# The second batch's queries loaded between the context pieces of the first batch, in a three-part transformer kernel on one core

## The chip, the cores and the metric

The kernel runs on one core of a Trainium2 chip. The metric is the device time of one execution in microseconds, the median of several executions. Times inside the kernel come from one profiled execution, counted from the start of its span.

## The reference

The program computes three sublayers in float32 on `x`, 8 batches of 64 rows of 2048. What matters here is the first of them:

```python
def _L0_xattn_ref(query, key):
    a = jnp.einsum('bqd,bkd->bqk', query, key)
    e = jax.nn.softmax(a, axis=-1)
    c = jnp.einsum('bqk,bkd->bqd', e, key)
    return c

x = x + _L0_xattn_ref(_layernorm(x, axis=-1), ctx_4096)
x = x + _L0_attn_ref(_layernorm(x, axis=-1), w_q, w_k, w_v, w_o)
x = x + _L0_ffn_ref(_layernorm(x, axis=-1), A_w, B_w, Wq_w, keys)
```

The context `ctx_4096` has 8 batches of 1601 rows of 2048; it serves as keys and as values. The second sublayer is a causal self-attention with 32 query and 8 key heads, the third a gated low-rank feed-forward; the change touches neither.

## The kernel before, in words

**Cross attention.** A batch's 1601 context rows are split into two halves of 833 and 768 rows (`TILES`), and a half is a stage, so there are 16 stages. The 2048 columns are split into four pieces of 512. Piece (x, c) is half x, columns c; it is one buffer `raw[x][:, c]` in SBUF with a semaphore of its own, `raw_in[x][c]`. A stage takes eight steps (`PER`), two per piece. At step t TensorE transposes two 128-column chunks of the half (`transpose_step`, line 637), one for ScalarE and one for VectorE to copy out of PSUM into `ct` (lines 445 and 587), and then multiplies the queries with the chunks that step t-1 transposed (`scores`, lines 673 and 676). Before the transposes of step t TensorE waits until both copies of step t-1 are done (lines 716 and 717). From the second stage on the steps also carry the products of the probabilities with the stage before's context (line 703). Steps 0 to 7 work on half 0 of batch 0, steps 8 to 15 on half 1.

**Queries.** `xq` holds a batch's 64 rows of `x`. For batch 0 VectorE normalizes them at once; TensorE transposes them behind the transposes of step 0 (`first_queries`, line 658, which adds one to `first_q_done`), and ScalarE copies them out (line 422). After that `xq` is free for batch 1. VectorE takes up a next batch's queries inside its loop over the steps of the batch before: after the copies of steps 3 and 4 the row statistics (`STATS_AT`, line 489, half of the columns in each), at steps 5 and 6 the chain for the inverse root, at steps 7 and 8 the normalization (line 499). At step 3 it first waits for the load:

```python
                    if at == STATS_AT[0]:
                        dve.wait_ge(xq_in, 16 * (b + 2))
```

The statistics of step 3 stand in VectorE's program behind the copy of step 3 and ahead of the copy of step 4. TensorE transposes the new queries at steps 13 and 14 (`Q_AT`, line 646).

**Loads.** All loads are issued by SyncE in program order (`cross_sync`, lines 363 to 418), on one queue. It issues the queries of batch 0, then the eight pieces of batch 0 in the order (0,0) to (0,3), (1,0) to (1,3), each from the third on after the piece two before it has landed, then the residual rows `xr` (the same rows of `x`, added to the output of the attention), and then it goes through the steps. At step 1 it waits for `first_q_done` and issues the queries of batch 1. A piece of half 0 takes three DMAs (128 partitions, 64 partitions and one row), a piece of half 1 one, `load_rows` one. Pieces of batch 1 are issued as the products of batch 0 release the buffers.

**The rest.** The decoder (self-attention and feed-forward, from line 800 on) follows on each engine behind the cross attention. Its first weight loads are issued at steps 100 and 106.

Of the kernel before, what the change touches and what calls it, by code (L numbers as in the profile page):

```python
# [16 lines left out]
NCOL = D // 512  # L17
# [82 lines left out]
def groups_before(t, ago):  # L100

    return GROUPS_AT.get(t - ago, [])
# [26 lines left out]
def evacuations(t):  # L129

    return min(t, STEPS) + 1
# [93 lines left out]
def cross_attention(nc, stack, x_rows, ctx, x1, x1_norm, ps, ident, ident_ready, x1_tiles, x1_ahead, row_bn,  # L225
# [5 lines left out]
    def keys_of(b, x, c, k0, k1, p0, p):  # L231
        lo = KEY0[x] + k0 * P + p0
        return ctx[b, lo:lo + (k1 - k0) * p, c * 512:(c + 1) * 512].rearrange("(k p) n -> p k n", p=p)
# [3 lines left out]
    def sb(name, shape, dt=F32):  # L237
        size = 4
        for n in shape[1:]:
            size *= n  # L240
        t = nc.alloc_sbuf_tensor_at(name, shape, dt, offset=here[0])
        here[0] += (size + 31) // 32 * 32
        return t

    def sem(name):
        return stack.enter_context(nc.semaphore(name))
# [3 lines left out]
    xq = sb("xa_xq", [P, D])[0:LQ, :]  # L250
# [36 lines left out]
    xq_in = sem("xa_xq_in")  # L287
# [5 lines left out]
    first_q_done = sem("xa_first_q_done")  # L293
# [24 lines left out]
    def column(c):  # L318
        return slice(c * 512, (c + 1) * 512)
# [8 lines left out]
    def both(eng, sems, n):  # L328

        for s in sems:  # L330
            eng.wait_ge(s, n)

    def group_over(h, c):
        return uses_before(h) + GROUP_END[h % HALVES][c] + 1
# [28 lines left out]
    def cross_sync(sp, aside):  # L363
        def load_piece(b, x, c):
            for k0, k1, p0, p in loads[x]:
                sp.dma_start(raw[x][p0:p0 + p, c, k0:k1, :], keys_of(b, x, c, k0, k1, p0, p)).then_inc(raw_in[x][c], 16)

        def load_rows(b, dst, s):
            sp.dma_start(dst[:], x_rows[b * LQ:(b + 1) * LQ, :]).then_inc(s, 16)

        load_rows(0, xq, xq_in)
        order = [(x, c) for x in range(HALVES) for c in range(NCOL)]
        for n, (x, c) in enumerate(order):
            if n >= 2:
                px, pc = order[n - 2]
                sp.wait_ge(raw_in[px][pc], 16 * len(loads[px]))
            load_piece(0, x, c)
        load_rows(0, xr, xr_in)
        for t in range(ALL_STEPS):
            if t == 1:  # L380
                sp.wait_ge(first_q_done, 1)
                load_rows(1, xq, xq_in)
            if t % (HALVES * PER) == Q_AT[1] + 1:
                b = t // (HALVES * PER) + 1
                if b + 1 < B:
                    both(sp, t_done, evacuations(t - 1))
                    load_rows(b + 1, xq, xq_in)
            for h, c in groups_before(t, 1):
                b, x = divmod(h, HALVES)
                both(sp, pv_done, group_over(h, c))  # L390
                if b + 1 < B:
                    load_piece(b + 1, x, c)
                elif x == 0 and c == 0:
                    for i in range(NCOL):
                        sp.wait_ge(stored[i], 16 * (B - 1))
                    sp.dma_start(x1_tiles[RT - 1][0:LQ, :], x1[(B - 2) * LQ:(B - 1) * LQ, :]).then_inc(sixth_in, 16)
                elif x == 0 and c == 1:
                    sp.wait_ge(norm_stored, 16 * (B - 2))
                    for r in range(RT - 1):
                        sp.dma_start(x1_ahead[r][:], x1_norm[r * P:(r + 1) * P, :]).then_inc(ahead_in[r], 16)  # L400
            for h, c in groups_before(t, 2):
                b, x = divmod(h, HALVES)
                if x == 1 and b + 1 < B:
                    sp.wait_ge(finished, NCOL * b + c + 1)
                    sp.dma_start(x1[b * LQ:(b + 1) * LQ, column(c)], xr[:, column(c)]).then_inc(stored[c], 16)
            if t in STORE_AT:
                b = STORE_AT[t]
                sp.wait_ge(out_norm, 2 * (b + 1))
                sp.dma_start(x1_norm[b * LQ:(b + 1) * LQ, :], xr[:]).then_inc(norm_stored, 16)
            if t in NEXT_AT:  # L410
                b = NEXT_AT[t]
                if b < B - 2:
                    sp.wait_ge(norm_stored, 16 * (b + 1))
                for c in range(NCOL):
                    sp.wait_ge(stored[c], 16 * (b + 1))
                load_rows(b + 1, xr, xr_in)
            if t in WEIGHT_LOAD_AT:
                aside(sp, WEIGHT_LOAD_AT.index(t))
# [313 lines left out]

    over = Over(pv_done, uses_before(STAGES), finished, ahead_in, stored)
    return over, (cross_sync, cross_scalar, cross_vector, cross_tensor)


# [1013 lines left out]
```

## Time and profile before

| | before |
|---|---|
| median of 3 executions | 1733.93 us (1732.92 to 1733.97) |
| profiled execution: device time | 1732.88 us |
| profiled execution: span | 1731.1 us |
| TensorE (PE) matmul busy | 1670.8 us |
| VectorE (DVE) busy | 560.9 us |
| ScalarE (ACT) busy | 455.4 us |
| GpSimd (POOL) busy | 372.5 us |
| mean granted clock of TensorE | 0.992 |

The span runs from the first to the last recorded instruction; the device time has a little more around it. PE are matmuls and transposes (a transpose is a matmul against the identity), SPq is SyncE's queue of DMA issues. In a timeline a row is a run of like instructions: start, duration, engine, line, operation, tiles, count, and in brackets the idle time before it with what ended it. A granted clock of 1.00 is 2.4 GHz, 0.50 is 1.2 GHz.

### The profile page before, as it was taken

How to read it: one execution, taken by the hardware profiler on the slowest of the kernel's cores; microseconds unless marked ns; L12 is line 12 of the kernel's file. 1: busy time of each engine (PE TensorE's matmuls, PEld its weight loads, DVE VectorE, ACT ScalarE, POOL GpSimd, SP SyncE). 2: the span in 40 equal slices, each digit the busy share in tenths (PEclk: the TensorE clock that was granted, in tenths of full speed). 3: DMA queues.
4: the chain of work that ended last, by engine and by line, in shares of the span. 5: the costliest groups of instructions: out<-in, count | busy, mean ns of one | idle time of the engine just before them, and what ended most of it. 6: DMA issues, size and time to landing. Idle time of an engine off the chain costs nothing.

```text
span 1731.1 us, 21539 instructions
## 1 busy us (share of the span) xinstructions
PE 1670.8 (97%) x9037; PEld 1224.9 (71%) x9037; DVE 560.9 (32%) x1018; ACT 455.4 (26%) x630; POOL 372.5 (22%) x95
## 2 busy tenths in 40 slices
PE   4899999999999979999999999999999999999999
PEld 3555555555555538888888878888888788887877
DVE  2445546365463451101202202103012022138423
ACT  1223332333333323231121221222212212232221
POOL 0000000000001002434434344343443443350010
PEclk9899999999999999999999999999999999999999
DMA  9166665757677543323233223223223342220023
GB/s 335 46 198 193 209 209 187 225 171 232 194 225 244 173 136 122 98 73 97 75 95 97 76 94 97 77 93 96 90 88 88 97 145 74 98 98 25 25 73 122
DMA packets 178882, 224.51 MB, mean 130 GB/s; under 512 B 4240, under 2 KB 102544, under 8 KB 176048
## 3 DMA queue, kind: packets, MB, share of 16 engines
q1 hardware_dynamic: 178816, 223.56, 40.9%
q8 instruction: 50, 0.82, 0.2%
q14 instruction: 16, 0.13, 0.0%
HBM read 212.54 MB, written 11.01 MB: 129 GB/s over the span
## 4 chain that ended last, share of the span: by engine, by line
PE 93%; DMA 2%; DVE 2%; ACT 1%; issue 1%; SPq 0%; DVEq 0%; ACTq 0%
PE ps L763 19%; PE ps L765 18%; PE ps L764 18%; PE ps L637 11%; PE ps L673 10%; PE ps L703 10%; PE ps L1487 2%; PE ps L1601 1%; DMA xa_raw_a<-in_ctx 1%; PE ps L1508 1%; DMA xa_xq<-in_x 1%; PE ps L646 1%; PE ps L1456 0%; DMA xa_raw_b<-in_ctx 0%; PE ps L1494 0%
## 5 line engine op out<-in xcount | busy, mean ns | idle before, releaser
L1071 POOL TENSOR_TENSOR w_lo<-raw,w_hi 128x2048 fp32r<-128x2048 f32 x75 | 345.1, 4602 | 647.8 <-ACT w_hi L1123 647.8
L763 PE MATMUL ps<-h_hi,w_hi 128*128 128x512 f32 x800 | 316.8, 396 | 0.0
L765 PE MATMUL ps<-h_hi,w_lo 128*128 128x512 f32 x800 | 312.1, 390 | 0.0
L764 PE MATMUL ps<-h_lo,w_hi 128*128 128x512 f32 x800 | 312.0, 390 | 0.0
L1307 DVE TENSOR_TENSOR rows<-rows,ps 128x512 f32<-128x512 f32 x128 | 87.9, 687 | 427.5 <-PE ps L765 427.5
L763 PE MATMUL ps<-w_hi,o_hi 128*128 128x512 f32 x528 | 208.1, 394 | 6.1 <-ACT sa_q_t L1158 4.1
L587 DVE COPY xa_ct<-ps 128x768 f32<-128x768 f32 (+1 forms) x128 | 126.8, 990 | 258.0 <-PE ps L637 174.1
L1123 ACT ACTIVATE w_hi<-raw 128x2048 fp32r<-128x2048 f32 x75 | 143.5, 1914 | 240.4 <-PE ps L765 240.4
L765 PE MATMUL ps<-w_hi,o_lo 128*128 128x512 f32 x528 | 205.8, 390 | 0.0
L764 PE MATMUL ps<-w_lo,o_hi 128*128 128x512 f32 x528 | 205.7, 390 | 0.0
L673 PE MATMUL ps<-xa_ct,xa_q_t 128*64 128x384 f32 x1024 | 203.3, 508 | 0.0
L445 ACT ACTIVATE xa_ct<-ps 128x768 f32<-128x768 f32 (+1 forms) x128 | 107.3, 838 | 331.0 <-PE ps L637 228.6
L763 PEld LDWEIGHTS ps<-h_hi,w_hi 128*128 128x128 f32 x800 | 150.6, 188 | 34.5 <-ACT sa_v_t L1158 2.0
L765 PEld LDWEIGHTS ps<-h_hi,w_lo 128*128 128x128 f32 x800 | 150.4, 188 | 31.8
L764 PEld LDWEIGHTS ps<-h_lo,w_hi 128*128 128x128 f32 x800 | 150.7, 188 | 29.8
L637 PEld LDWEIGHTS ps<-ident,xa_raw_a 128*128 128x128 f32 (+1 forms) x896 | 98.9, 145 | 74.8 <-issue 72.3
L637 PE MATMUL ps<-ident,xa_raw_a 128*128 128x128 f32 (+1 forms) x896 | 111.6, 276 | 28.7 <-DVE xa_ct L587 15.2
L637 PEld LDWEIGHTS ps<-ident,xa_raw_b 128*128 128x128 f32 x768 | 82.8, 140 | 59.3 <-issue 54.8
L1076 POOL TENSOR_TENSOR w_lo<-raw,w_hi 128x2048 fp32r<-128x2048 f32 x2 | 9.4, 4698 | 535.2 <-ACT w_hi L986 535.2
L763 PEld LDWEIGHTS ps<-w_hi,o_hi 128*128 128x128 f32 x528 | 99.2, 188 | 29.4 <-ACT sa_q_t L1158 6.7
L765 PEld LDWEIGHTS ps<-w_hi,o_lo 128*128 128x128 f32 x528 | 99.2, 188 | 20.8
L764 PEld LDWEIGHTS ps<-w_lo,o_hi 128*128 128x128 f32 x528 | 99.3, 188 | 19.7
(205 smaller groups left out, 1530.4 us busy)
## 6 DMA issues: line engine op xcount, KB each, us to landing
xa_raw_a<-in_ctx SPq DMA_DIRECT2D x32, 1536.0 KB
xa_raw_b<-in_ctx SPq DMA_DIRECT2D x32, 1536.0 KB, 6.7
raw<-in_L_attn_w_q SPq DMA_DIRECT2D x32, 1024.0 KB, 5.6
raw<-in_L_attn_w_o SPq DMA_DIRECT2D x30, 1024.0 KB, 5.0
raw<-in_L_attn_w_k SPq DMA_DIRECT2D x8, 1024.0 KB, 5.5
raw<-in_L_attn_w_v SPq DMA_DIRECT2D x8, 1024.0 KB, 5.2
xa_xq<-in_x SPq DMA_DIRECT2D x8, 512.0 KB, 8.3
xa_raw_a<-in_ctx SPq DMA_DIRECT2D x32, 128.0 KB
```

The source lines that it names most:

```text
L445: ins = act.activation(ct[:, t % 2, 0, 0:width(t)], ps_t[:, 0, 0:width(t)], ACT.Copy)
L587: ins = dve.tensor_copy(ct[:, t % 2, 1, 0:width(t)], ps_t[:, 1, 0:width(t)])
L637: ins = pe.transpose(ps_t[:, u, k * P:k * P + p], raw[x][0:p, c, k, g % 4 * P:(g % 4 + 1) * P], ident[0:p, 0:p])
L673: ins = [pe.matmul(ps_s[side(a), bank, 0:MAIN], q, keys[:, a * MAIN:(a + 1) * MAIN], start=first, stop=last) for a in range(SIDES)]
L703: pe.matmul(group_bank(h, col)[side(a), :], pe_lhs, tile, start=start, stop=stop).then_inc(pv_done[a], 1)
L763: pe.matmul(out, hi, mov_hi, start=first, stop=False)
L764: pe.matmul(out, hi, mov_lo, start=False, stop=False)
L765: return pe.matmul(out, lo, mov_hi, start=False, stop=last)
L1071: pool.tensor_tensor(w_lo[:, n, :], raw[:, n, :], w_hi[:, n, :].bitcast(F32), ALU.subtract).then_inc(w_lo_done, 1)
L1123: act.activation(w_hi[:, n % 2, :], raw[:, n % 2, :], ACT.Copy).then_inc(w_hi_done, 1)
L1307: dve.tensor_tensor(part, part, ps_mm[:, n % 2, :], ALU.add).then_inc(wo_added, 1)
L1487: i = pe.matmul(ps_s[:, (2 * r + hp) * 2 + b2, :], q_t[:, 2 * r + b2, 2 * hp:2 * hp + 2, :], k_t[:, q0:q0 + LQ], start=True, stop=True)
```

## The change

The wait for `first_q_done` and the load of batch 1's rows into `xq` leave the loop over the steps and go into the loop over the context pieces, behind the issue of the fourth of them, piece (0,3). Everything else stays, the order of the other loads too.

```diff
                 px, pc = order[n - 2]
                 sp.wait_ge(raw_in[px][pc], 16 * len(loads[px]))
             load_piece(0, x, c)
+            if n == NCOL - 1:
+                sp.wait_ge(first_q_done, 1)
+                load_rows(1, xq, xq_in)
         load_rows(0, xr, xr_in)
         for t in range(ALL_STEPS):
-            if t == 1:
-                sp.wait_ge(first_q_done, 1)
-                load_rows(1, xq, xq_in)
             if t % (HALVES * PER) == Q_AT[1] + 1:
```

## Rows read from the trace of the kernel before

**Rows 1.** The page: the span, and TensorE's busy time.

```profile
span 1731.1 us, 21539 instructions
PE 1670.8 (97%) x9037; PEld 1224.9 (71%) x9037; DVE 560.9 (32%) x1018; ACT 455.4 (26%) x630; POOL 372.5 (22%) x95
```

**Rows 2.** The chain of waits, 0 to 60 us: start us, us, what.

```profile
17.08 8.20 DMA xa_raw_a<-in_ctx
...
34.25 12.57 DMA xa_xq<-in_x
```

**Rows 3.** TensorE's waits, 0 to 60 us: us in total, times, longest.

```profile
PE ps L637 <- DVE xa_ct L587: 15.2, 1, 15.2
```

**Rows 4.** Timeline of TensorE, 0 to 110 us.

```profile
14.53 1.97 PE L658 MATMUL ps<-ident,xa_xq 64*128 64x64 f32 x16
...
24.39 1.65 PE L637 MATMUL ps<-ident,xa_raw_a 128*128 128x128 f32 x14
...
27.58 1.65 PE L637 MATMUL ps<-ident,xa_raw_a 128*128 128x128 f32 x14
...
30.77 1.65 PE L637 MATMUL ps<-ident,xa_raw_a 128*128 128x128 f32 x14
...
33.75 0.28 PE L676 MATMUL ps<-xa_ct,xa_q_t 128*64 128x65 f32 x2
49.19 3.01 PE L637 MATMUL ps<-ident,xa_raw_a 128*128 128x128 f32 x14 [15.16 <-DVE xa_ct L587]
...
55.16 1.65 PE L637 MATMUL ps<-ident,xa_raw_a 128*128 128x128 f32 x14
...
61.55 1.53 PE L637 MATMUL ps<-ident,xa_raw_b 128*128 128x128 f32 x12
...
68.43 0.84 PE L637 MATMUL ps<-ident,xa_raw_b 128*128 128x128 f32 x6 [0.84 <-ACT xa_ct L445]
```

**Rows 5.** Timeline of VectorE, 29 to 62 us.

```profile
29.27 1.02 DVE L587 COPY xa_ct<-ps 128x833 f32<-128x833 f32 x1 [2.17 <-PE ps L637]
46.84 1.28 DVE L489 BATCH_NORM_STATS2 xa_bn<-xa_xq 64x6 f32<-64x512 f32 x2 [16.55 <-DMA xa_xq<-in_x]
48.04 1.00 DVE L587 COPY xa_ct<-ps 128x833 f32<-128x833 f32 x1
...
60.11 1.02 DVE L587 COPY xa_ct<-ps 128x833 f32<-128x833 f32 x1 [0.97 <-PE ps L637]
61.06 0.98 DVE L499 TENSOR_SCALAR xa_xq<-xa_xq,xa_mv,xa_rs_w 64x512 f32<-64x512 f32 x2
```

**Rows 6.** Timeline of SyncE's queue, stretches between 15 and 35 us.

```profile
16.07 1.46 SPq L366 DMA_DIRECT2D xa_raw_a<-in_ctx  x3
...
20.66 12.95 SPq L366 DMA_DIRECT2D xa_raw_b<-in_ctx  x4
...
28.84 0.37 SPq L366 DMA_DIRECT2D xa_raw_b<-in_ctx  x1
...
33.65 0.55 SPq L369 DMA_DIRECT2D xa_xr<-in_x  x1
34.25 0.59 SPq L369 DMA_DIRECT2D xa_xq<-in_x  x1
```

**Rows 7.** Busy us by stretch: PE, PEld, DVE, ACT, POOL, granted clock, DMA share, GB/s.

```profile
24.39:34.03 9.64, 9.64 (x80) 6.98 (x78) 2.05 (x2) 2.60 (x3) 0.00 (x0) 1.00 1.03 392
...
36.00:38.00 2.00, 0.00 (x0) 0.00 (x0) 0.00 (x0) 0.00 (x0) 0.00 (x0) 1.00 1.04 403
38.00:40.00 2.00, 0.00 (x0) 0.00 (x0) 0.00 (x0) 0.00 (x0) 0.00 (x0) 0.52 1.12 415
...
41.00:42.00 1.00, 0.00 (x0) 0.00 (x0) 0.00 (x0) 0.00 (x0) 0.00 (x0) 0.50 0.99 203
...
49.19:55.16 5.97, 5.97 (x26) 4.14 (x26) 3.08 (x9) 0.87 (x1) 0.00 (x0) 0.50 0.00 0
```

**Rows 8.** TensorE's waits, 60 us to the end.

```profile
PE ps L1456 <- ACT normed L1132: 8.4, 1, 8.4
```

## The prediction

> **What bounds the kernel now.** Read the page first: TensorE is busy for 1670.8 of 1731.1 us [rows 1], so any gain must come from the 60 us in which it stands, or from stretches at the lower clock. The chain of waits of the first 60 us says where the largest piece is: from 34.25 on, 12.57 us of the chain belong to one transfer, `xa_xq<-in_x`, the second batch's queries [rows 2]. The list of TensorE's waits puts one wait of 15.2 us on a VectorE copy, line 587 [rows 3]. The timeline of TensorE shows it in the code's terms. A step of the cross attention begins with its transposes (line 637): step 2 at 24.39, step 3 at 27.58, step 4 at 30.77, so a step takes 3.19 us. Step 5 should begin at 33.96, and the work of step 4 does end at 34.03; step 5 begins at 49.19 [rows 4]. VectorE's timeline gives the reason: after its copy of step 3 (29.27, 1.02 us) it does nothing until 46.84, where the row statistics of the second queries begin; the copy that step 5 waits for stands behind them and runs at 48.04 [rows 5]. In the code VectorE waits at step 3 for `xq_in` (line 614), ahead of its copy of step 4. So this is no shortage of VectorE, but head of line: a wait for data that nobody needs before step 13 blocks a copy that is needed at once. SyncE's timeline shows why the data are late: it issues this load at 34.25, behind all eight context pieces and the residual rows of 33.65 [rows 6].
>
> **What the change does there.** The wait for `first_q_done` and the load move from behind the residual rows to right behind piece (0,3), the fourth. No instruction is added or removed. SyncE ends the three DMAs of piece (0,3) at 16.07 + 1.46 = 17.53 [rows 6]. The transposes whose end gives `first_q_done` end at 14.53 + 1.97 = 16.50 [rows 4], so the moved wait is met 1.0 us before SyncE gets to it. The load issues at 17.55, takes 0.59 us of SyncE, and SyncE is free again at 18.14. The next piece waits anyway for piece (0,2), until 20.66 (28.84 is the same wait two pieces on, [rows 6]); issue costs nothing.
>
> **When it lands.** Piece (0,3), issued just ahead of it, lands at 17.08 + 8.20 = 25.28 [rows 2]. The load is 0.52 MB. Where in the trace of before only the 64-row loads of `x` are left, the DMA engines are as busy as before but move about 203 GB/s [rows 7], against 392 GB/s with the context in between 24.39 and 34.03: 0.52 MB / 203 GB/s = 2.6 us, my estimate of its place in the queue. Served in order it lands at 25.28 + 2.6 = 27.9. The bounds: 25.3, should it be shared out beside piece (0,3), and 17.55 + 12.57 = 30.1, should it need as long from issue to landing as in the trace of before. I take 27.9; in the new place two pieces stand before it (one half done), as the trace's piece (0,3) had.
>
> **When it must be there.** In the trace of before step 5 begins 49.19 - 46.82 = 2.37 us after the landing [rows 2, 4] (half the statistics, then the copy). For step 5 to begin at 33.96 the load must land by 31.6. VectorE asks for it at 30.29, when the copy of step 3 ends. All three values lie before that: 1.5 us to spare at the worst bound, 3.7 us at the value taken. From there VectorE's own work fits into the steps: statistics 1.28 and a copy 1.02 are 2.3 us of 3.19, and the copy of 60.11 with half a normalization behind it (0.98) ran in just such a step without delay to TensorE, which took (61.55 - 55.16) / 2 = 3.20 us a step [rows 4, 5].
>
> **What TensorE gets back.** Two terms. First the stall: step 4 to step 5 takes 49.19 - 30.77 = 18.42 us and would take 3.19, which is 15.23 us. Second the clock: step 5 takes 55.16 - 49.19 = 5.97 us for the work of a 3.19 us step [rows 4]; its stretch ran at a granted clock of 0.50, the lower of the two levels (1.2 of 2.4 GHz), after an idle stretch in which the grant fell from 1.00 (36 to 38 us) to 0.52 (38 to 40 us) [rows 7]. Without the idle stretch there is no fall: 2.78 us. Together 18.01 us; step 8 begins at 43.5 instead of 61.55.
>
> **What it may cost.** The four pieces (1,0) to (1,3) and the residual rows now lie behind the load, each up to 2.6 us later. Piece (1,0) landed when SyncE went on, at 28.84 [rows 6], and is first wanted at step 8, now at 43.5: 14.7 us to spare, less 2.6. Piece (1,1) had landed when the eighth piece was issued, at about 33.2 (the four issues end at 20.66 + 12.95 = 33.61, one takes 0.37 [rows 6]); its step 10 begins at 68.43 - 18.0 = 50.4 [rows 4]. The last pieces follow at one step of two per piece, and the DMA engines drained everything by 46.8; the residual rows are wanted only where the batch's outputs are finished. Cost: 0. The other cover is bandwidth: steps 5 to 7 now run beside transfers. Steps 2 to 4 ran at 3.19 us beside 392 GB/s [rows 4, 7], steps 6 and 7 at 3.20 with the DMA idle [rows 4]: cost 0.
>
> **Does the rest move up whole?** All later loads, stores and weight loads are released by TensorE's progress or follow it, so their distances stay. TensorE's largest named wait after 60 us is 8.4 us, at the handover to the decoder, on work that comes after the cross attention [rows 8]. Nothing behind step 8 is tied to an absolute time. Passed on: 18.0 of 18.0 us.
>
> **The sum.** The profiled execution took 1732.88 us (span 1731.1 and 1.8 around it): 1732.88 - 18.0 = 1714.9. The median of the runs shown is 1.05 above it, 1733.93, so against the median 1715.9, which is my forecast. A measurement of this kernel can tell about 0.2% (3.5 us) from no change.
>
> **Rivals.** *A, landed late.* The load is spread so that it ends only with piece (1,1), which landed at about 33.2; with the load's own 2.6 us that is 35.8, or 4.2 us past 31.6. TensorE stands 4.2 us at step 5. The grant was still 1.00 at 36 to 38 us, two to four us after the idle time began [rows 7], so the clock may hold: gain 13.8, time 1720.1; with the clock lost too, gain 11.0, time 1722.9. For it speaks that `xq` took 12.57 us last time; against it that those included the residual rows and a tail of 64-row transfers. Chance 0.07.
>
> *B, slower: the clock does not hold.* With no idle stretch TensorE goes on with steps that are nearly half transposes, and the grant could fall to 0.50 in them. Each such step costs 5.97 - 3.19 = 2.78 us. The three steps 5 to 7 alone would take 8.3 us of the gain (1724.2); it ends slower than before from the seventh low step on (7 x 2.78 = 19.5, time 1735.4), that is if all steps from 5 to 11 run low. Against it: steps 2 to 4, of the same mix, kept 1.00 throughout [rows 7], and steps 6 and 7 full pace.
> The Trainium skill, "TensorE: Matmul & The Clock Gate", section "Part 4: PE-mode transpose", says that transposes do not count as busy for the clock in the way that matmuls do. By that rule this change, which packs transposes without rest, could lose clock; the trace does not bear it out where transposes and score matmuls alternate. Chance of a slower result 0.02, of a partly eaten gain 0.02.
>
> *C, no effect.* Some other late work takes the place of the wait at step 5, for example ScalarE's half of the copies. But its copy of step 4 stands behind no such wait, and TensorE's list of the first 60 us has no second wait on that step. Time 1733.9; chance 0.01.
>
> **Chances and range.** The full gain 0.88, A 0.07, B 0.04, C 0.01. Faster by over 0.2%: the full gain, A, and the part of B that keeps a gain, 0.97; within 0.2% 0.01; slower 0.02. The range reaches down to 1713.5 (the sum against the profiled execution, 1714.9, with 1.4 us for the step times and the scatter, 1 us in the runs shown) and up to 1720.5, A with the clock kept; that leaves out A with the clock lost, B and C.
>
> **What would show it.** Right: the 15.2 us wait is gone from TensorE's list; step 5 begins near 34.0 and step 8 near 43.5; the granted clock is 1.00 from 24 to 60 us; SyncE issues the query load near 17.6 and VectorE's wait for it at step 3 is zero, its statistics beginning near 30.3; the eighth piece is issued up to 2.6 us later than 33.2. Wrong: a new wait of TensorE on line 587 at step 5 (A), a granted clock under 1.00 in steps 5 to 11 (B), a wait on a context piece at step 8 or later, or a longer wait at the decoder's beginning that takes back what the start gave.

## The result and the profile after

The changed kernel took 1715.62 us (median of 4 executions, 1714.56 to 1717.68) against 1733.95 us for the kernel before. The ratio is 0.9894, with a 95% interval of 0.9877 to 0.9912. Run once more beside the last experiments it took 1714.39 us against 1732.33, ratio 0.9900 (0.9885 to 0.9915). The profiled execution took 1715.08 us, 17.8 less than the one of before. The forecast was 1715.9. That it lies only 0.3 us off is partly luck: the four executions spread over 3.1 us, and the medians of the changed kernel, taken twice, differ by 1.2 us.

The page's lines that answer to [rows 1]:

```profile
span 1713.3 us, 21539 instructions
PE 1668.4 (97%) x9037; PEld 1222.4 (71%) x9037; DVE 561.0 (33%) x1018; ACT 455.5 (27%) x630; POOL 372.5 (22%) x95
```

TensorE does the same work in 2.4 us less busy time (1670.8 to 1668.4: work at the lower clock that is gone). The rest of the 17.8 us was idle time.

TensorE's waits from 0 to 60 us, the whole list (for [rows 3]; us in total, times, longest):

```profile
PE ps L637 <- DMA xa_raw_a<-in_ctx: 11.4, 1, 11.4
PE ps L637 <- ACT xa_q_t L422: 1.9, 1, 1.9
PE ps L637 <- ACT xa_ct L445: 0.8, 1, 0.8
```

The 15.2 us on line 587 are gone, and nothing took their place. The waits for the first piece and for the transposed queries were there before too (11.6 and 1.9 us). The 0.8 us on line 445 stood at step 10 before as well [rows 4]. TensorE's timeline from step 0 on, for [rows 4] (step 1 is the 18.20, step 5 the 33.54, step 8 the 43.12, step 10 the 50.01):

```profile
14.32 1.97 PE L658 MATMUL ps<-ident,xa_xq 64*128 64x64 f32 x16
18.20 3.01 PE L637 MATMUL ps<-ident,xa_raw_a 128*128 128x128 f32 x14 [1.92 <-ACT xa_q_t L422]
...
23.97 1.65 PE L637 MATMUL ps<-ident,xa_raw_a 128*128 128x128 f32 x14
...
30.35 1.65 PE L637 MATMUL ps<-ident,xa_raw_a 128*128 128x128 f32 x14
...
33.54 1.65 PE L637 MATMUL ps<-ident,xa_raw_a 128*128 128x128 f32 x14
...
36.74 1.65 PE L637 MATMUL ps<-ident,xa_raw_a 128*128 128x128 f32 x14
...
43.12 1.53 PE L637 MATMUL ps<-ident,xa_raw_b 128*128 128x128 f32 x12
...
50.01 0.85 PE L637 MATMUL ps<-ident,xa_raw_b 128*128 128x128 f32 x6 [0.84 <-ACT xa_ct L445]
```

Steps 2 to 7 run one behind the other at 3.19 us. VectorE's timeline shows the statistics directly behind the copy of step 3, with no idle time ahead of them, for [rows 5]:

```profile
28.85 1.03 DVE L587 COPY xa_ct<-ps 128x833 f32<-128x833 f32 x1 [2.17 <-PE ps L637]
29.79 1.27 DVE L489 BATCH_NORM_STATS2 xa_bn<-xa_xq 64x6 f32<-64x512 f32 x2
32.04 1.03 DVE L587 COPY xa_ct<-ps 128x833 f32<-128x833 f32 x1 [0.98 <-PE ps L637]
```

SyncE's queue, for [rows 6]: the load goes out at 17.51, behind piece (0,3), and the four issues of half 1 end at 20.74 + 15.81 = 36.55, 2.94 us later than before (33.61):

```profile
16.01 1.46 SPq L366 DMA_DIRECT2D xa_raw_a<-in_ctx  x3
17.51 0.48 SPq L369 DMA_DIRECT2D xa_xq<-in_x  x1
20.74 15.81 SPq L366 DMA_DIRECT2D xa_raw_b<-in_ctx  x4
36.59 0.56 SPq L369 DMA_DIRECT2D xa_xr<-in_x  x1
```

SyncE issues piece (1,1) as soon as piece (0,3) has landed, and (1,2) as soon as (1,0) has. The queue's rows for these two issues:

```profile
26.06 0.37 SPq L366 DMA_DIRECT2D xa_raw_b<-in_ctx  x1
...
32.61 0.37 SPq L366 DMA_DIRECT2D xa_raw_b<-in_ctx  x1
```

So piece (0,3), issued ahead of the load, landed at 26.06 and not at 25.3 as before, and piece (1,0) at 32.6 and not at 28.84 [rows 6].

The stretches of [rows 7] (busy us of PE, PEld, DVE, ACT, POOL; granted clock, DMA share, GB/s): the DMA's rate fell from 392 to 332 GB/s in the stretch with the 64-row load, and the grant stays at 1.00 where it had fallen.

```profile
24.39:34.03 9.64, 9.64 (x81) 7.05 (x79) 5.23 (x7) 2.60 (x3) 0.00 (x0) 1.00 1.01 332
...
36.00:38.00 2.00, 2.00 (x20) 1.62 (x18) 1.34 (x7) 0.29 (x1) 0.00 (x0) 1.00 1.05 410
38.00:40.00 2.00, 2.00 (x18) 1.14 (x16) 1.43 (x4) 0.57 (x1) 0.00 (x0) 1.00 1.05 381
```

The wait at the decoder's beginning [rows 8] is unchanged, so nothing was given back there:

```profile
PE ps L1456 <- ACT normed L1132: 8.4, 1, 8.4
```

### The profile page after: what moved, and what is told of

It is laid out like the page before. It is cut to its first block, busy times and chain, and to the rows that moved or that the text cites. A ratio compares the mean times of both kernels' runs of the same rounds, so it can differ in the third digit from the quotient of the medians.

```text
span 1713.3 us, 21539 instructions
## 1 busy us (share of the span) xinstructions
PE 1668.4 (97%) x9037; PEld 1222.4 (71%) x9037; DVE 561.0 (33%) x1018; ACT 455.5 (27%) x630; POOL 372.5 (22%) x95
## 4 chain that ended last, share of the span: by engine, by line
PE 95%; DVE 2%; ACT 1%; issue 1%; DMA 1%; SPq 0%; DVEq 0%; ACTq 0%
PE ps L763 19%; PE ps L765 18%; PE ps L764 18%; PE ps L637 12%; PE ps L673 11%; PE ps L703 10%; PE ps L1487 2%; PE ps L1601 1%; PE ps L1508 1%; PE ps L646 1%; DMA xa_raw_a<-in_ctx 1%; PE ps L1456 0%; PE ps L1494 0%; PE ps L676 0%; PE ps L649 0%
```

## The experiments

None of the twelve kernels leaves out work. In each row below the ratio is to the kernel before, run beside it. The profile of a kernel is one of its executions, and not always a typical one: those of q_after_piece8 (1729.93 us), fill_transposes (1730.31) and warm_change (1713.10) lie 1.9 to 3.5 us under the medians of their kernels, that of fill_shorter (1737.12) 3.7 us over it.

| kernel | median us | ratio (95% interval) |
|---|---|---|
| q_after_piece5 | 1717.51 | 0.9911 (0.9895 to 0.9928) |
| q_after_piece6 | 1723.5 | 0.9947 (0.9931 to 0.9964) |
| q_after_piece7 | 1727.84 | 0.9971 (0.9959 to 0.9982) |
| q_after_piece8 | 1732.01 | 0.999 (0.9981 to 1.0) |
| stats_later | 1718.64 | 0.9921 (0.9905 to 0.9938) |
| residual_early | 1714.59 | 0.9891 (0.9874 to 0.9907) |
| fill_transposes | 1732.19 | 0.9999 (0.9989 to 1.0008) |
| fill_matmuls | 1743.51 | 1.0062 (1.0045 to 1.0079) |
| change_again | 1714.39 | 0.99 (0.9885 to 0.9915) |
| fill_shorter | 1733.38 | 1.0006 (0.9996 to 1.0015) |
| warm_change | 1716.55 | 0.9908 (0.9893 to 0.9924) |
| warm_before | 1733.23 | 1.0008 (0.9999 to 1.0017) |

**The same load, one piece later each time.** From the changed kernel, with 4, 5, 6 and 7 for n:

```diff
-            if n == NCOL - 1:
+            if n == 4:
```

> The query load goes one piece later, behind the fifth piece (1,0). Theory (head of line: TensorE loses what the load lands after 31.2 us, measured as 2.4 us before step 5 may begin at 33.54): piece (1,0) landed at about 28.8 before, the load adds the 2.9 us that it took in the changed kernel, so it lands at 31.7; step 5 begins 0.3 to 0.8 us late, no clock lost, time within 1 us of the changed kernel's 1715.6. Rival (the gain comes from an emptier DMA queue at the end, not from the landing): it lies an even fifth of the way back, about 1719.

> The query load goes behind the sixth piece (1,1). Theory: it lands at 33.2 + 2.9 = 36.1, TensorE stands until about 38.5, a stall of 4.7 us; whether the clock holds is open, since before it was still granted in full 4 us after TensorE stopped and gone by 6: 1715.6 + 4.7 = 1720.3 with the clock, 1723.1 without (2.8 us more). This is the price of the prediction's rival A. Rival (queue end): about 1723 whatever the clock does, with no stall of that size at step 5.

> The query load goes behind the seventh piece (1,2). Theory: it lands at 37.3 + 2.9 = 40.2, the stall is 8.8 us and the clock falls, so step 5 takes 5.97 us: 1715.6 + 8.8 + 2.8 = 1727.2. If the clock were no term of its own, 1724.4.

> The query load goes behind the eighth piece (1,3) but still ahead of the residual rows; against the kernel before only those rows are moved out of its way. Theory: it lands at 41.4 + 2.9 = 44.3, 2.5 us earlier than before, so the stall is 12.7 us and the clock falls: 1715.6 + 12.7 + 2.8 = 1731.1, 2.8 us under the kernel before. Rival (the residual rows were the whole obstacle): near 1716.

The landing is the issue plus the time to landing in each profile. A step is given by the start of its transposes:

| load behind piece | issued | landed | step 4 | step 5 | step 6 | landing to step 5 | TensorE idle | step 5 lasts |
|---|---|---|---|---|---|---|---|---|
| 4th (the change) | 17.51 | 28.2 | 30.35 | 33.54 | 36.74 | (not what it waits for) | 0 | 3.20 |
| 5th | 20.61 | 32.2 | 28.45 | 34.59 | 39.37 | 2.4 | 2.87 | 4.78 |
| 6th | 24.97 | 37.2 | 28.75 | 39.55 | 44.09 | 2.4 | 7.54 | 4.54 |
| 7th | 29.41 | 42.3 | 30.31 | 44.70 | 50.67 | 2.4 | 11.13 | 5.97 |
| 8th | 32.99 | 43.9 | 29.41 | 46.23 | 50.91 | 2.3 | 13.55 | 4.68 |
| residual rows (before) | 34.25 | 46.8 | 30.77 | 49.19 | 55.16 | 2.4 | 15.16 | 5.97 |

Step 5 begins 2.3 to 2.4 us behind the landing in all five kernels that are late, and the medians climb with it: 1717.5, 1723.5, 1727.8, 1732.0. That is the head-of-line theory. The medians alone do not decide against the rival of an emptier queue end, whose even fifths (1719.3, 1722.9, 1726.6 and 1730.3) lie within 2 us of them. What decides is the stall at step 5, which the rival does not have, and the next experiment, which leaves the queue as it was. The residual rows were not the obstacle: with the load ahead of them but behind all pieces the gain is 0.1%, with an interval that reaches to none.

The stalls came out larger than expected: 2.87, 7.54, 11.13 and 13.55 us against 0.3 to 0.8, 4.7, 8.8 and 12.7. Three of the landings were later than expected (32.2, 37.2 and 42.3 against 31.7, 36.1 and 40.2), and in three of the profiles TensorE reached step 4 0.9 to 1.9 us sooner than in the changed kernel's, which lengthens the stall but not the execution. At the fifth place the expectation failed: the time was to stay within 1 us of 1715.6 and is 1.9 us over it. There step 4 began at 28.45, 1.9 us sooner, the load landed 0.5 us late, and the clock, which was to hold, fell. TensorE's timeline and the stretches:

```profile
28.45 1.65 PE L637 MATMUL ps<-ident,xa_raw_a 128*128 128x128 f32 x14
34.59 2.76 PE L637 MATMUL ps<-ident,xa_raw_a 128*128 128x128 f32 x14 [2.87 <-DVE xa_ct L587]
...
39.37 1.66 PE L637 MATMUL ps<-ident,xa_raw_a 128*128 128x128 f32 x14
```

```profile
34.60:36.00 1.40, 1.40 (x9) 1.40 (x10) 1.04 (x2) 0.01 (x1) 0.00 (x0) 0.60 1.04 405
36.00:37.00 1.00, 1.00 (x6) 1.00 (x5) 0.00 (x0) 0.86 (x1) 0.00 (x0) 0.50 1.06 414
```

After 2.87 us without work the grant went to 0.50 when TensorE was already at work again, and step 5 took 4.78 us in place of 3.19.

**The consumer moved and not the load.** The kernel before, with VectorE's work on the next queries moved to later steps:

```diff
-STATS_AT, CHAIN_AT, NORM_AT = (3, 4), (5, 6), (7, 8)
+STATS_AT, CHAIN_AT, NORM_AT = (8, 9), (9, 10), (11, 12)
```

> The kernel before with its order of loads untouched; VectorE instead takes up the next batch's queries later: statistics at steps 8 and 9 (was 3 and 4), the chain for the inverse root at 9 and 10 (was 5 and 6), the normalization at 11 and 12 (was 7 and 8). Theory (TensorE never needed the data, only the copy queued behind the wait): the load still lands at 46.8, VectorE meets its wait at step 8, near 46 us, and stands for at most 1 or 2 us; the 15.2 us wait is gone and the time is near 1716, plus what the new places cost in each of eight batches (0 to 8 us). Rival (the early transfer itself is what helps, by an emptier queue or otherwise): near 1734.

The load was issued at 34.09 and landed at 45.9, as late as ever, and TensorE did not stop: its steps 2 to 8 follow each other at 3.19 us, step 8 at 41.60. VectorE's timeline from the copy of step 8 on shows no idle time ahead of the statistics; the load had landed at 45.9, and in between stand the row maxima of the scores (lines 516 to 524):

```profile
43.17 0.96 DVE L587 COPY xa_ct<-ps 128x768 f32<-128x768 f32 x1 [2.04 <-PE ps L637]
...
46.54 1.27 DVE L489 BATCH_NORM_STATS2 xa_bn<-xa_xq 64x6 f32<-64x512 f32 x2
47.73 0.93 DVE L587 COPY xa_ct<-ps 128x768 f32<-128x768 f32 x1
```

So TensorE never needed the queries this early, only the copy behind the wait. The ratio is 0.9921, a little over the change's 0.9894, with intervals that overlap. The new places have a small price: after 60 us TensorE's waits on line 637 without a releaser are 8.5 us instead of 5.8, and 1.7 us on VectorE's normalization (line 499) are new. From step 8 to the decoder's first transposes it takes 619.59 - 41.60 = 577.99 us, against 617.19 - 43.12 = 574.07 in the changed kernel.

**The delay of the context pieces doubled.** The changed kernel, with the residual rows' load right behind the query load (`+` is the same line, indented into the loop):

```diff
                 load_rows(1, xq, xq_in)
-        load_rows(0, xr, xr_in)
+                load_rows(0, xr, xr_in)
```

> The changed kernel, and the residual rows' load moved too, to right behind the query load, ahead of the four pieces of half 1. This doubles the delay of those pieces. Theory (they have 12 us and more to spare): SyncE issues the last piece about 3 us later than in the changed kernel, near 39, TensorE shows no wait on a piece, and the time stays at 1715.6 within 1 us. Rival (the pieces are near their need): TensorE waits at step 8 and the time rises by up to 3 us.

```profile
16.61 0.48 SPq L369 DMA_DIRECT2D xa_xq<-in_x  x1
17.13 0.60 SPq L369 DMA_DIRECT2D xa_xr<-in_x  x1
19.60 18.49 SPq L366 DMA_DIRECT2D xa_raw_b<-in_ctx  x4
```

SyncE's queue ends the last piece's issue at 38.09, not near 39. Its four issues take 18.49 us from first to last, against 15.81 in the changed kernel and 12.95 before [rows 6], so their delay did double. TensorE shows no wait on a piece of half 1, and the ratio (0.9891) is within the interval of the change. The pieces have room.

**The clock as a term of its own.** The kernel before, with filler ahead of TensorE's wait of step 5. The second kernel has `pe.matmul` in place of `pe.transpose`, the third 100 transposes in place of 130:

```diff
+            if t == 5:
+                for _ in range(130):
+                    pe.transpose(ps[:, 7, 0:P], ident[:], ident[:])
             if has_transposes(t):
```

> The kernel before, with 130 transposes of the identity (128x128, into an idle PSUM bank) put on TensorE ahead of its wait of step 5, about 14.7 us of work at 0.113 us each. Theory (the clock is a term of its own, 2.8 us): VectorE's wait and the landing stay, step 5 begins near 49.2 as before, but its 3.19 us are not stretched to 5.97, so the time is 1731.1. Rival (transposes don't hold the clock): the grant falls to 0.50 under them, they take about twice as long each, the filler itself runs past 49 us and the time is 1740 or more.

> The same with 130 matmuls of the identity in place of the transposes, same shapes. Theory: as with transposes, step 5 runs in 3.2 us at a grant of 1.00 and the time is 1731.1, if a matmul of this shape takes 0.113 us as a transpose does; if it takes up to four times as long, the filler passes 49 us and adds what it passes it by. Rival (the clock falls whatever TensorE does in a stall of 15 us): 1733.9 or more, step 5 at 5.97 us.

> The kernel before with 100 transposes of the identity ahead of TensorE's wait of step 5, in place of 130: 11.1 us of filler, which ends about 4 us before the copy is done in a run like the first profile. With 130 the filler ended only 1.2 us before the copy, so where an execution starts later it runs into step 5. Theory (the clock is a term of its own): step 5 takes 3.2 us and the ratio to the kernel before is 0.9984, 2.8 us. Rival (what the clock gives back is lost elsewhere): step 5 at full pace, but a ratio of 1.000 within 0.0005.

TensorE's timeline with 130 transposes:

```profile
32.79 14.41 PE L715 MATMUL ps<-ident 128*128 128x128 f32 x130
48.40 1.62 PE L637 MATMUL ps<-ident,xa_raw_a 128*128 128x128 f32 x14 [1.21 <-DVE xa_ct L587]
51.57 1.65 PE L637 MATMUL ps<-ident,xa_raw_a 128*128 128x128 f32 x14
```

and two of its stretches, in the filler and in step 5:

```profile
38.00:40.00 2.00, 2.00 (x21) 2.00 (x20) 0.00 (x0) 0.00 (x0) 0.00 (x0) 1.00 1.12 429
...
50.00:52.00 2.00, 2.00 (x17) 1.25 (x17) 1.72 (x6) 0.21 (x1) 0.00 (x0) 1.00 0.00 0
```

Step 5 is still held until 2.4 us behind the landing, but with the stall filled the grant stays at 1.00 and step 5 takes 51.57 - 48.40 = 3.17 us, not 5.97. The mechanism is shown. In this profile the gain also reaches the decoder, which begins at 632.01, 3.59 us earlier than before: 2.80 by the shorter step 5 and 0.79 because step 5 began sooner. But the 2.8 us do not show in the timed total: the ratio is 0.9999 with an interval down to 0.9989, and the forecast of 0.9984 lies outside it. A fit between filler and copy of only 1.21 us in the profile may not hold in every execution; that is argued. The shorter filler was to settle this. Its timed ratio of 1.0006 (from 0.9996) excludes 0.9984 too. Its profile does not show the reason, because it had a late landing (49.2), with the DMA engines at 360 GB/s between 33 and 41 us, against 397 to 420 GB/s between 33 and 40 us in the kernel before:

```profile
33.25 11.14 PE L715 MATMUL ps<-ident 128*128 128x128 f32 x100
51.56 3.01 PE L637 MATMUL ps<-ident,xa_raw_a 128*128 128x128 f32 x14 [7.17 <-DVE xa_ct L587]
```

TensorE stood for 7.17 us after the filler and the grant was 0.50 by 48 us. So neither timed comparison gives the clock term back, and how much of it a typical execution pays stays open. In the five stalled kernels step 5 lost 1.4 to 2.8 us to it (4.54 to 5.97 against 3.19). The matmul filler says little on this: a matmul of this shape is two records of 0.113 us each, 260 in all, so the filler took 29.3 us and ran to 60 us, 11 us past 49, and the kernel was 11 us (0.6%) slower, as its expectation allows. Its grant was 1.00 from 30 to 58 us.

**A head start, with and without the stall behind it.** 60 transposes of the identity ahead of step 0, in the changed kernel and in the one before, beside one more run of the change:

```diff
         pe.wait_ge(ident_ready, 2)
+        for _ in range(60):
+            pe.transpose(ps[:, 7, 0:P], ident[:], ident[:])
```

> The changed kernel once more, in the same rounds as the three below. Theory: 18 us under the kernel before, as the first time. The start of step 2 will differ from 23.97 by up to 2.5 us, since the grant rose at different moments of step 1 in the runs so far (step 2 began between 21.3 and 24.0 us), and that difference should show in the start of step 5, 9.6 us behind it.

> The changed kernel with 60 transposes of the identity into an idle PSUM bank ahead of step 0, while TensorE waits for piece (0,0); they end by 9 us. Theory (transposes hold the clock, as the filler of step 5 showed, and nothing downstream is tied to a landing any more): steps 0 and 1 run at the higher level, step 0's transposes take 1.65 us and not 3.0 (hidden by the wait for the queries), the query transposes 1.2 and not 2.0, step 1 3.2 and not 5.8: 3.0 to 3.5 us less than the changed kernel, near 1712.3, unless the load's landing at 28.2 catches up: step 5 would want to begin at 30.2, the landing allows 30.6. Rival (the wait of VectorE comes back): the head start is lost to the landing, and less than 1 us is left.

> The same 60 transposes in the kernel before. Theory: steps 0 to 4 end 3 us earlier, but step 5 still begins 2.4 us after the landing at 46.8, so the stall grows by what the start gains and the time is the same within 0.5 us (ratio 1.000). Rival (gains add up whatever stands behind them): 3 us less, ratio 0.998.

In the kernel before, steps 2 and 4 begin earlier (20.76 and 27.21 against 24.39 and 30.77), and all of it goes into the stall (18.25 us against 15.16):

```profile
27.21 1.65 PE L639 MATMUL ps<-ident,xa_raw_a 128*128 128x128 f32 x14
48.73 3.01 PE L639 MATMUL ps<-ident,xa_raw_a 128*128 128x128 f32 x14 [18.25 <-DVE xa_ct L587]
```

Ratio 1.0008: no gain, as expected. In the changed kernel the head start meets the landing again:

```profile
26.48 1.65 PE L639 MATMUL ps<-ident,xa_raw_a 128*128 128x128 f32 x14
31.22 1.62 PE L639 MATMUL ps<-ident,xa_raw_a 128*128 128x128 f32 x14 [1.48 <-DVE xa_ct L587]
```

The load had landed at 28.9 (17.77 + 11.1), and step 5 began 2.3 us behind it. 3 us were expected, unless the landing caught up, and it did. Step 8 began at 40.77, against 40.95 in the repeat of the change beside it and 43.12 in its first profile, and the median is not lower (1716.55 against 1714.39). So the head start gained nothing. The profile explains part of that: in the repeat, with no help, step 1 took 4.79 us instead of 5.77 and step 2 began at 21.79. Why the other three executions of warm_change took 1716.35 to 1717.25 us is not shown; the one in the profile took 1713.10.

Nor did the head start hold the clock in both kernels. In the changed one step 1 took 3.17 us. In the kernel before it took 20.76 - 16.11 = 4.65 us, with a grant of 0.50 from 18 to 20 us, behind the same wait of 1.92 us for the queries' copy.

## Why the prediction was right

**Where the time was lost.** Right: one wait of VectorE for data that are not needed yet, ahead of a copy that is. The experiment that moved only the consumer confirms it on the other side.

**The load's landing.** Forecast 27.9 with bounds 25.3 to 30.1, measured 17.51 + 10.7 = 28.2. The two parts of that sum erred in opposite ways: piece (0,3) landed at 26.06 and not at 25.28, and the load 2.1 us behind it and not 2.6. So it is not shown that the load was served strictly behind the piece.

**The pieces behind it.** The last of them was issued 2.94 us later in this pair of profiles, over the 2.6 us that the prediction gave as the most. Other profiles scatter by as much: from the first issue of half 1 to the last it is 15.2 to 15.6 us in the three with the query load alone in that place, and 12.6 to 14.4 us in the seven with no load of rows ahead of these issues. The middle values differ by 2.3 us. None of it matters here, because TensorE waited for none of these pieces.

**The moved wait on `first_q_done`.** Free, as forecast: the transposes ended at 14.32 + 1.97 = 16.29, and SyncE issued at 17.51.

**The deadline.** Landing to step 5 was read as 2.37 us from one case; five kernels give 2.3 to 2.4. The room for the landing was called 3.7 us. In the profile after, it is 33.54 - 2.4 - 28.2 = 2.9. It is smaller where TensorE starts sooner: 1.8 in the repeat (31.37 - 2.4 - 27.2), gone in the warmed kernel. The forecast took TensorE's arrival for fixed, and it is not.

**The two terms.** Stall 15.23 and clock 2.78, 18.01 in all, measured as 61.55 - 43.12 = 18.43 at step 8, of which 0.42 is an earlier step 2 (23.97 against 24.39), so 18.01 for the change in this pair of profiles. That the 2.78 are a typical figure was an assumption: the term scatters between 1.4 and 2.8 us in the stalled kernels, and the two fillers of transposes did not win it in the timed total. The ratio of the change does not settle it: the stall of 15.23 us alone would give 0.9912, which is the edge of the first interval and within that of the repeat. So the stall is confirmed in the profiles and in the timed ratios, the clock term in the profiles only.

**Passed on whole.** The first transposes of the decoder (line 1456) begin at 617.19 instead of 635.60, 18.41 us earlier. From there to the end it is 1713.3 - 617.19 = 1096.1 against 1095.5 before; these 0.6 us are the difference to the 17.8 us of the spans. In the repeat the decoder begins 2.19 us earlier still and the rest takes 1097.5. In the fourteen profiles this last part takes 1095.5 to 1098.7 us and does not follow the time at which it begins, so these 0.6 us are scatter.

**The rivals.** *A* did not come about, but the runs priced it. Its place in the table is the sixth piece: forecast 1720.1 with the clock held and 1722.9 without, measured 1723.5. The parts differ from its own, 7.54 us of stall and 1.35 of clock against 4.2 and 2.8, because TensorE reached step 4 2.0 us sooner and the load landed 1.4 us later than *A* had it. Its hope that the clock holds over a 4 us stall has nothing left for it, since the grant fell over one of 2.87. *B* is out: the grant was 1.00 through steps 5 to 7. The Trainium skill, "TensorE: Matmul & The Clock Gate", section "Part 4: PE-mode transpose", says that transposes do not count as busy in the way that matmuls do. Here 130 of them back to back, and nothing else, kept the grant at 1.00 for 14.41 us, so the measurement decides against that for this shape. A step is 1.65 us of transposes in 3.19, a little over half and not nearly half, as *B* had it. *C* is out with the list of waits.

## What to carry to other kernels

When the busiest engine waits for another engine's copy, look at what stands ahead of that copy in the other engine's program. If it is a wait for data that are needed much later, either load them earlier or take them up later; both removed the stall here, and the later place cost about 4 us of it elsewhere. Work out the deadline for such a load from the latest landing that the critical engine tolerates, and keep room in it for executions in which that engine arrives sooner. Time saved ahead of a stall that ends with a transfer goes into the stall.

## What the hardware showed that was not expected

The start of step 2 lay between 20.1 and 24.4 us in all profiles together, and between 21.3 and 24.4 without the warm-up. In those twelve, step 0 began at 10.5 to 11.6 (the landing of the first piece), the query transposes took 1.24 to 1.97 us, and step 1 4.75 to 5.97 us. A step at full pace takes 3.19, so the lower clock costs a different amount each time. The column of the granted clock can't be relied on there: in the profiles before and after it reads 1.00 from the start, while the 14 transposes of steps 0 and 1 take 3.01 us each time, as they do at 0.50 in step 5 [rows 4], and 1.65 at full pace. In the stalled kernels that scatter is absorbed by the wait for the landing.

The grant fell to 0.50 with TensorE already at work behind a stall of 2.87 us, but stayed at 1.00 over one of 1.48 us. Behind a wait of 1.92 us it fell in warm_before and not in warm_change. Behind a long stall the same step 5 took anything from 4.54 to 5.97 us.

A load of 64 rows moves about 203 GB/s with the DMA engines fully busy [rows 7], against 392 with the context's 128-row tiles: 0.52 MB of it cost the pieces behind it 2.94 us in the first pair of profiles and 2.3 us by the middle values of all.
